# A router chain's scratch in PSUM, its gate folded away, and the norms' small steps on another engine

## The chip, the core and the metric

One core of a Trainium2 chip runs the whole program. TensorE (PE in the rows) multiplies matrices into PSUM, eight banks of 2 KB per partition; VectorE (DVE) and ScalarE (ACT) compute from SBUF or PSUM; GpSimd (POOL) computes from SBUF; SyncE (SP) issues transfers. The metric is device microseconds of one launch, lower is better.

## The reference

The input x is 8 batches of 512 channels by 2048 positions, in float32. Two layers, each added to x through a gate:

```python
x = x + tanh(g_xattn[0]) * xattn(layernorm(x), ctx, mask, ...)
x = x + tanh(g_ffn[0]) * ffn(layernorm(x), router_weight, router_bias, expert_bias)
```

xattn: windows of 128 positions; q and k from the normalised x (512 to 256 channels), v from ctx, 8 heads of 32, softmax, times v, exact gelu, back to 512 channels. ffn, for each of the 4096 rows of a length of 2048:

```python
logits = flat @ router_weight.T + router_bias          # 64 experts
scores = softmax(logits)
topk_w, topk_idx = top_k(scores, 8)
w_sum = topk_w.sum(-1, keepdims=True)
w_dense = zeros.at[rows, topk_idx].add(topk_w)
out = flat * w_sum + w_dense @ expert_bias
```

With flat = (x - m) * rstd, the second layer is x * (1 + t*w_sum*rstd) - t*w_sum*rstd*m + t*(w_dense @ expert_bias), with t = tanh(g_ffn). The factor, the shift and the mix are what the lines around the change compute.

## The kernel before

A unit is 256 positions of one batch: 8 units a batch, 64 in all. The order of all work is written as a table of lags, SLOTS: a unit starts every 16 slots, and each engine walks through the same ticks (8 to a slot) and emits what is due. A batch takes 128 slots. ENDS shifts the last units. Each engine has its own instruction stream in this order, and semaphores join them.

For a unit, GpSimd normalises x to z32 (z_full, L1051), ScalarE rounds it to z_hi, GpSimd takes the rest z_lo (z_low, L1058), and TensorE makes q and k from three products each (L310 to L312). ctx is split likewise (cx_hi L599, cx_lo L1064), and v_mm (L325 to L327) makes v, which ScalarE takes out of PSUM (v_full, L605). Scores (L341, L349), row maxima (top, L766), exponentials (L615, in four groups), transposes of P in 32x32 blocks on VectorE (turn_p, L773), the denominators (L778, L782), sixteen transfers that regroup the blocks to PT (move, L521; SyncE waits there for the division of the unit before), the product with v (L366), the division (divide, L788), gelu (L631), a split into ot_hi (L640) and ot_lo (L1075), the output projection (L385 to L387), its evacuation (L801) and GpSimd's add into x (L1070). Then the new x is transposed (L404), split (L647, L831) and multiplied by the router weights into the bank PR (L417, L418); bn_stats (L814) gathers mean and variance.

Once per batch, after its last unit, comes the router chain, amid the work of the next batch's first units. norm2 on VectorE: bn_aggr (L819), the negated mean (L823), variance plus eps (L824); on GpSimd the power -0.5 (L1079), which gives rstd in ln2[:, 2, :]. c_gate on VectorE: gate[0] = rstd * tanh(g_ffn) (L839) and gate[1] = gate[0] * -mean (L841). ScalarE copies PR to L (c_logits, L653), TensorE turns it into a bank called LT (c_turn, L428), of which the first 256 of 512 columns are used. c_top: logits times rstd plus bias (L847), the eight largest (L852), negation of the largest (L857), marking of the eight (match_replace L859, not_equal L862) in the SBUF tile lr. ScalarE takes the exponentials (c_exp, L658). c_weights: reciprocal of the sum (L866), masked weights (L868), normalised and doubled into w2 (L872). c_scale: sum of the weights (L877), times the two gates (L880, L881), plus one (L883), which signals ac. TensorE transposes w2 (w_turn, L439), ScalarE and VectorE split it (wt_hi L665, wt_lo L889), ScalarE scales x (L673), TensorE mixes the expert biases (L454, L455), VectorE adds (add_mix, L900), SyncE stores (L531) and later loads the batch after next (L526).

The statistics of the next batch's input go the same way: bn_aggr (L922), negated mean and variance plus eps on VectorE (L926, L927), the power on GpSimd (L1084).

Seven PSUM banks form a ring. take() gives each product the bank that is planned to be free first, by the table's due times, and notes the semaphore and count of that bank's last reader; TensorE waits for just this before it writes. So the planned end of a bank's use changes which bank the next products get and whom they wait for:

```python
at, i, last_reader, k = min(free)
...
free.append((t + round(8 * held), i, freed_by, n))
```

## Time and profile before

| | us |
|---|---|
| median of 3 runs | 1210.87 |
| lowest, highest | 1206.91, 1213.17 |
| profiled execution | 1210.61 |
| its span | 1208.5 |

| engine | busy us | share |
|---|---|---|
| TensorE, matmuls | 1126.1 | 93% |
| ScalarE | 1029.2 | 85% |
| VectorE | 975.5 | 81% |
| GpSimd | 707.7 | 59% |

The span's mean granted clock of TensorE was 0.985 of full speed. Matmuls are pipelined, so their busy time is not time at their peak; where TensorE stands still is read from its waits. A duration of an instruction includes the time that it stands after it has started. In a timeline a row can be several instructions of one line (x3), and the note in brackets is the engine's idle time before it and what ended it. SPq rows are SyncE's issuing of transfers.

### The profile page before, as it was taken

To read this page: it belongs to the slowest core of one execution; us is meant where nothing else is said; L and a number is where in the kernel's file an instruction comes from. 1 tells how busy PE (TensorE), PEld (TensorE's weight loads), DVE (VectorE), ACT (ScalarE), POOL (GpSimd) and SP (SyncE) were. 2 spreads that over 40 slices of the span, in tenths; PEclk is the share of its full clock that TensorE was granted. 3 is DMA by queue.
4 is the path that set the end of the run, shared out by engine and by line. 5 is a ranking of instruction groups with operands and counts; after the bars stand their busy time and mean duration, and the time that the engine had idled before them with its cause. 6 is when DMAs were issued, how large, how long until landed. Compare 5 with 4: busy or idle time off the path is not lost.

```text
span 1208.5 us, 33324 instructions
## 1 busy us (share of the span) xinstructions
PE 1126.1 (93%) x11661; PEld 1046.1 (87%) x11661; DVE 975.5 (81%) x1882; ACT 1029.2 (85%) x3200; POOL 707.7 (59%) x660
## 2 busy tenths in 40 slices
PE   2699999989999899999999999999999989999977
PEld 2699999889988899898998999988998889989965
DVE  6658878988789777998779887898779977797757
ACT  4688999888989799988998889898998879998954
POOL 2366677466655577466764666746764647746621
PEclk9899999999999999999999999999999989999989
DMA  9267554775548844487556965478554884456433
GB/s 287 74 175 199 143 130 116 237 201 155 132 112 252 218 124 123 117 270 209 131 129 187 235 169 131 119 233 217 141 131 121 253 215 124 125 137 203 110 92 139
DMA packets 169766, 199.82 MB, mean 165 GB/s; under 512 B 27776, under 2 KB 104704, under 8 KB 169472
## 3 DMA queue, kind: packets, MB, share of 16 engines
q1 hardware_dynamic: 168448, 197.20, 59.8%
q8 instruction: 93, 1.52, 0.6%
q10 hardware_dynamic: 1152, 0.50, 0.2%
q14 instruction: 73, 0.60, 0.2%
HBM read 80.06 MB, written 33.65 MB: 94 GB/s over the span
## 4 chain that ended last, share of the span: by engine, by line
PE 56%; SPq 21%; DVE 10%; issue 4%; ACT 4%; DMA 3%; POOL 1%; DVEq 0%; ACTq 0%; POOLq 0%
SPq L521 13%; PE ring L310 7%; PE ring L312 7%; PE ring L311 7%; DVE X L900 4%; PE ring L366 4%; SPq L526 4%; PE ring L325 3%; PE ring L327 3%; PE ring L326 3%; PE ring L349 3%; PE ring L385 3%; PE ring L387 3%; PE ring L386 3%; PE ring L404 3%
## 5 line engine op out<-in xcount | busy, mean ns | idle before, releaser
L615 ACT ACTIVATE P<-ring,nmx 128x128 f32<-128x128 f32 x1024 | 358.6, 402 | 30.9 <-DVE nmx L766 30.3
L310 PE MATMUL ring<-z_hi,wqk_hi 128*128 128x256 f32 x1024 | 299.8, 293 | 24.3 <-DVE z_lo L965 22.0
L311 PE MATMUL ring<-z_hi,wqk_lo 128*128 128x256 f32 x1024 | 292.4, 286 | 0.0
L312 PE MATMUL ring<-z_lo,wqk_hi 128*128 128x256 f32 x1024 | 292.3, 285 | 0.0
L615 ACT ACTIVATION_READ_ACCUMULATOR P<-ring,nmx 128x1 f32 x1024 | 248.5, 243 | 0.0
L1058 POOL TENSOR_TENSOR z_lo<-z,z_hi 128x1024 fp32r<-128x1024 f32 x62 | 147.6, 2381 | 167.5 <-ACT z_hi L583 167.5
L310 PEld LDWEIGHTS ring<-z_hi,wqk_hi 128*128 128x128 f32 x1024 | 198.5, 194 | 37.2 <-DVE wqk_lo L940 21.9
L1070 POOL TENSOR_TENSOR X<-X,xt 128x512 f32<-128x512 f32 x128 | 165.5, 1293 | 67.7 <-DVE xt L801 67.6
L773 DVE STREAM_TRANSPOSE T<-P 128x512 f32<-128x512 f32 x256 | 169.2, 690 | 44.2 <-ACT P L615 24.0
L311 PEld LDWEIGHTS ring<-z_hi,wqk_lo 128*128 128x128 f32 x1024 | 198.9, 194 | 0.0
L312 PEld LDWEIGHTS ring<-z_lo,wqk_hi 128*128 128x128 f32 x1024 | 198.9, 194 | 0.0
L1064 POOL TENSOR_TENSOR cx_lo<-cx,cx_hi 128x512 fp32r<-128x512 f32 x128 | 165.1, 1290 | 38.8 <-ACT cx_hi L599 38.7
L1075 POOL TENSOR_TENSOR ot_lo<-o,ot_hi 128x512 fp32r<-128x512 f32 x63 | 81.5, 1294 | 165.7 <-ACT ot_hi L640 165.7
L766 DVE TENSOR_REDUCE nmx<-ring 128x4 f32<-128x512 f32 x256 | 158.6, 682 | 16.7 <-PE ring L349 16.7
L325 PE MATMUL ring<-wv_hi,cx_hi 128*128 128x256 f32 x512 | 146.3, 286 | 8.1 <-POOL cx_lo L1064 8.1
L385 PE MATMUL ring<-ot_hi,wo_hi 128*128 128x256 f32 x504 | 143.1, 284 | 10.7 <-POOL ot_lo L1075 10.7
L801 DVE SCALAR_TENSOR_TENSOR xt<-ring,cst,mg 128x256 f32<-128x256 f32 x256 | 111.4, 477 | 45.0 <-PE ring L387 42.9
L326 PE MATMUL ring<-wv_lo,cx_hi 128*128 128x256 f32 x512 | 145.4, 284 | 0.0
L327 PE MATMUL ring<-wv_hi,cx_lo 128*128 128x256 f32 x512 | 145.4, 284 | 0.0
L387 PE MATMUL ring<-ot_lo,wo_hi 128*128 128x256 f32 x504 | 142.7, 283 | 0.0
L386 PE MATMUL ring<-ot_hi,wo_lo 128*128 128x256 f32 x504 | 142.2, 282 | 0.0
L1051 POOL TENSOR_SCALAR z<-X,ln 128x256 f32<-128x256 f32 x252 | 137.7, 562 | 0.7
(137 smaller groups left out, 2697.3 us busy)
## 6 DMA issues: line engine op xcount, KB each, us to landing
PT<-T SPq DMA_DIRECT2D x1018, 80.0 KB, 2.1
cx<-in_ctx SPq DMA_DIRECT2D x128, 256.0 KB, 3.9
out_y<-X SPq DMA_DIRECT2D x128, 256.0 KB, 3.1
X<-in_x SPq DMA_DIRECT2D x112, 256.0 KB, 4.6
mg<-in_mask SPq DMA_DIRECT2D x64, 128.0 KB, 3.2
X<-in_x SPq DMA_DIRECT2D x8, 512.0 KB, 8.5
sel<-rows_d SPq DMA_DIRECT2D x256, 3.0 KB
X<-in_eb SPq DMA_DIRECT2D x2, 512.0 KB, 7.7
```

The source lines that it names most:

```text
L310: e.matmul(o, wqk_hi[:, t, cols], z_hi[:, t, :], t == 0, False)
L311: e.matmul(o, wqk_lo[:, t, cols], z_hi[:, t, :], False, False)
L312: last = e.matmul(o, wqk_hi[:, t, cols], z_lo[:, t, :], False, t == DT - 1)
L325: e.matmul(o, cx_hi[:, k, :], wv_hi[:, k, :], k == 0, False)
L326: e.matmul(o, cx_hi[:, k, :], wv_lo[:, k, :], False, False)
L327: last = e.matmul(o, cx_lo[:, k, :], wv_hi[:, k, :], False, k == DT - 1)
L385: e.matmul(o, wo_hi[:, m, cols], o_hi[:, m, :], m == 0, False)
L386: e.matmul(o, wo_lo[:, m, cols], o_hi[:, m, :], False, False)
L387: last = e.matmul(o, wo_hi[:, m, cols], o_lo[:, m, :], False, m == 1)
L615: last = e.activation(P[:, n, :], bank("S", 4 * u + g)[:, k * W:(k + 1) * W], ACT.Exp, bias=nmx[u % 2][:, n:n + 1], accum_out=den[u % 2][: ...
L773: e.transpose(T[u % 2][:, :, 4 * g:4 * g + 4, :].rearrange("p b k i -> p k b i"), P[:, 4 * g:4 * g + 4, :].rearrange("p k (b j) -> p k b j ...
L1070: e.tensor_tensor(xs, xs, xt[j][:], ALU.add).then_inc(x1_g, 1)
```

## The change

The tile lr goes: the marks of the eight largest and the masked weights are written to the unused half of the logits' bank LT, low(b), and c_scale's two intermediate results to the bank's first columns. So LT is held until ac instead of lg: in the plan until c_sc (40.75) instead of c_top (38.75).

c_gate goes with its two instructions. c_scale forms the gain t * w_sum * rstd by one scalar_tensor_tensor from w_sum, tanh(g_ffn) and rstd, and the shift by another from the gain, -1 and the mean. It still has four instructions.

The negations of the mean and the additions of eps leave VectorE. In norm2 GpSimd adds eps before the power, and the negated mean is no longer formed. In input_norm GpSimd adds eps, negates the mean into nm1, and takes the power; z is still x plus the negated mean, times rstd. mv has two buffers now. Everything not shown below follows from this: names of semaphores, the place in the ticks where c_gate stood, and the operands of z (nm1 and rs1 for ln).

```diff
-    norm2=27.5, c_gate=33.5, L=36, LT=34, c_top=38.75, c_exp=37.75, c_w=40.75, c_sc=40.75, wT=43, wt_hi=43.25, wt_lo=42.25, mix=43.75, m_gap=0.25,
+    norm2=27.5, L=36, LT=34, c_top=38.75, c_exp=37.75, c_w=40.75, c_sc=40.75, wT=43, wt_hi=43.25, wt_lo=42.25, mix=43.75, m_gap=0.25,
...
-        mv = sb("mv", [128, DT, 2])
+        mv = [sb(f"mv{i}", [128, DT, 2]) for i in range(2)]
         bn2 = sb("bn2", [128, DT, 4, 6])
         mv2 = sb("mv2", [128, DT, 2])
-        ln1 = [sb(f"ln1_{i}", [128, 3, DT]) for i in range(2)]
-        ln2 = sb("ln2", [128, 3, DT])
+        rs1 = [sb(f"rs1_{i}", [128, DT]) for i in range(2)]
+        nm1 = [sb(f"nm1_{i}", [128, DT]) for i in range(2)]
+        rs2 = sb("rs2", [128, DT])
...
-        lr = sb("lr", [128, DT, NX])
...
-        gate = sb("gate", [128, 2, DT])
...
             for b in batch(t, C["LT"]):
-                take(("LT", b), t, C["c_top"] - C["LT"], lg_v, b + 1)
+                take(("LT", b), t, C["c_sc"] - C["LT"], ac_v, b + 1)
...
             def norm2(b):
                 e.wait_ge(bn2_v, 16 * (b + 1))
+                if b:
+                    e.wait_ge(ac_v, b)
                 for t in range(DT):
                     e.bn_aggr(mv2[:, t, :], bn2[:, t, :, :].rearrange("p a c -> p (a c)")).then_inc(agg2_v, 1)
-                if b:
-                    e.wait_ge(ac_v, b)
-                e.wait_ge(agg2_v, DT * (b + 1))
-                e.tensor_scalar(ln2[:, 0, :], mv2[:, :, 0], -1.0, None, ALU.mult).then_inc(neg2_v, 1)
-                e.tensor_scalar(ln2[:, 1, :], mv2[:, :, 1], EPS, None, ALU.add).then_inc(neg2_v, 1)
...
-            def c_gate(b):
+            def c_top(b):
                 if b == 0:
                     e.wait_ge(sm_rb, 16)
                     e.wait_ge(sm_small, 96)
-                e.wait_ge(neg2_v, 2 * b + 2)
-                e.wait_ge(rstd2_g, b + 1)
-                e.tensor_scalar(gate[:, 0, :], ln2[:, 2, :], cst[:, TF:TF + 1], None, ALU.mult).then_inc(dm_v, 1)
-                e.wait_ge(dm_v, b + 1)
-                e.tensor_tensor(gate[:, 1, :], gate[:, 0, :], ln2[:, 0, :], ALU.mult).then_inc(gate_v, 1)
-
-            def c_top(b):
                 e.wait_ge(rstd2_g, b + 1)
                 e.wait_ge(lt_pe, b + 1)
                 for t in range(DT):
                     last = e.scalar_tensor_tensor(out=lg[:, t, :], in0=bank("LT", b)[:, t * NX:(t + 1) * NX],
-                                                  scalar=ln2[:, 2, t:t + 1], in1=rbb[:], op0=ALU.mult, op1=ALU.add)
+                                                  scalar=rs2[:, t:t + 1], in1=rbb[:], op0=ALU.mult, op1=ALU.add)
                 last.then_inc(lg_v, 1)
                 e.wait_ge(lg_v, b + 1)
                 for t in range(DT):
...
                 e.wait_ge(t8_v, b + 1)
                 e.tensor_scalar(sc[:, :, 0:1], t8[:, :, 0:1], -1.0, None, ALU.mult).then_inc(neg_v, 1)
                 for t in range(DT):
-                    last = e.match_replace(lr[:, t, :], t8[:, t, :], lg[:, t, :], -3.0e38)
+                    last = e.match_replace(low(b)[:, t, :], t8[:, t, :], lg[:, t, :], -3.0e38)
                 last.then_inc(mr_v, 1)
                 e.wait_ge(mr_v, b + 1)
-                e.tensor_tensor(lr[:], lr[:], lg[:], ALU.not_equal).then_inc(sel_v, 1)
+                e.tensor_tensor(low(b), low(b), lg[:], ALU.not_equal).then_inc(sel_v, 1)
+
+            def low(b):
+                return bank("LT", b)[:, DT * NX:2 * DT * NX].rearrange("p (t x) -> p t x", t=DT)
 
             def c_weights(b):
                 e.wait_ge(ex_a, b + 1)
                 e.reciprocal(sc[:, :, 3:4], sc[:, :, 1:2]).then_inc(wm_v, 1)
                 e.wait_ge(sel_v, b + 1)
-                e.tensor_tensor(ex[:], ex[:], lr[:], ALU.mult).then_inc(wm_v, 1)
+                e.tensor_tensor(low(b), low(b), ex[:], ALU.mult).then_inc(wm_v, 1)
                 if b:
                     e.wait_ge(wT_pe, b)
                 e.wait_ge(wm_v, 4 * b + 2)
-                e.tensor_tensor(w2[:], ex[:].unsqueeze(2).to_broadcast([128, DT, 2, NX]),
+                e.tensor_tensor(w2[:], low(b).unsqueeze(2).to_broadcast([128, DT, 2, NX]),
                                 sc[:, :, 3:4].unsqueeze(3).to_broadcast([128, DT, 2, NX]), ALU.mult).then_inc(w2_v, 1)
 
             def c_scale(b):
                 e.wait_ge(w2_v, b + 1)
-                e.tensor_reduce(sc[:, :, 5:6], w2[:, :, 0, :], AX.X, ALU.add).then_inc(wm_v, 1)
-                e.wait_ge(gate_v, b + 1)
+                wsum, gain = bank("LT", b)[:, 0:DT], bank("LT", b)[:, DT:2 * DT]
+                e.tensor_reduce(wsum, w2[:, :, 0, :], AX.X, ALU.add).then_inc(wm_v, 1)
                 e.wait_ge(wm_v, 4 * b + 3)
-                e.tensor_tensor(sc[:, :, 4:5], sc[:, :, 5:6], gate[:, 0, :].unsqueeze(2), ALU.mult).then_inc(wm_v, 1)
-                e.tensor_tensor(sc[:, :, 7:8], sc[:, :, 5:6], gate[:, 1, :].unsqueeze(2), ALU.mult)
+                e.scalar_tensor_tensor(out=gain, in0=wsum, scalar=cst[:, TF:TF + 1], in1=rs2[:], op0=ALU.mult,
+                                       op1=ALU.mult).then_inc(wm_v, 1)
                 e.wait_ge(wm_v, 4 * b + 4)
-                e.tensor_scalar(sc[:, :, 6:7], sc[:, :, 4:5], 1.0, None, ALU.add).then_inc(ac_v, 1)
+                e.scalar_tensor_tensor(out=sc[:, :, 7], in0=gain, scalar=-1.0, in1=mv2[:, :, 0], op0=ALU.mult, op1=ALU.mult)
+                e.tensor_scalar(sc[:, :, 6], gain, 1.0, None, ALU.add).then_inc(ac_v, 1)
 
             def w_low(b):
...
             def input_norm(b):
-                ln = ln1[b % 2]
                 e.wait_ge(bn1_v, 16 * (b + 1) - 4)
-                if b:
-                    e.wait_ge(rstd1_g, b)
                 if b >= 2:
                     e.wait_ge(z32_g, NU * (b - 1) + 1)
                 for t in range(DT):
                     if b or t != TA:
-                        e.bn_aggr(mv[:, t, :], bnst[:, t, :, :].rearrange("p a c -> p (a c)")).then_inc(agg1_v, 1)
-                if b == 0:
-                    e.wait_ge(st_a, 6)
-                e.wait_ge(agg1_v, DT * (b + 1) - 1)
-                e.tensor_scalar(ln[:, 0, :], mv[:, :, 0], -1.0, None, ALU.mult).then_inc(neg1_v, 1)
-                e.tensor_scalar(ln[:, 1, :], mv[:, :, 1], EPS, None, ALU.add).then_inc(neg1_v, 1)
+                        e.bn_aggr(mv[b % 2][:, t, :], bnst[:, t, :, :].rearrange("p a c -> p (a c)")).then_inc(agg1_v, 1)
...
             def norm2(b):
-                e.wait_ge(neg2_v, 2 * (b + 1))
-                e.tensor_tensor(ln2[:, 2, :], ln2[:, 1, :], half[:], ALU.pow).then_inc(rstd2_g, 1)
+                e.wait_ge(agg2_v, DT * (b + 1))
+                e.tensor_scalar(rs2[:], mv2[:, :, 1], EPS, None, ALU.add).then_inc(eps2_g, 1)
+                e.wait_ge(eps2_g, b + 1)
+                e.tensor_tensor(rs2[:], rs2[:], half[:], ALU.pow).then_inc(rstd2_g, 1)
 
             def input_norm(b):
-                ln = ln1[b % 2]
-                e.wait_ge(neg1_v, 2 * (b + 1))
-                e.tensor_tensor(ln[:, 2, :], ln[:, 1, :], half[:], ALU.pow).then_inc(rstd1_g, 1)
+                if b == 0:
+                    e.wait_ge(st_a, 6)
+                e.wait_ge(agg1_v, DT * (b + 1) - 1)
+                e.tensor_scalar(rs1[b % 2][:], mv[b % 2][:, :, 1], EPS, None, ALU.add).then_inc(eps1_g, 1)
+                e.tensor_scalar(nm1[b % 2][:], mv[b % 2][:, :, 0], -1.0, None, ALU.mult).then_inc(eps1_g, 1)
+                e.wait_ge(eps1_g, 2 * b + 2)
+                e.tensor_tensor(rs1[b % 2][:], rs1[b % 2][:], half[:], ALU.pow).then_inc(rstd1_g, 1)
```

VectorE, around norm2 and c_gate of the second batch, with the semaphores that each row waits for. Before:

```order
338 L823 TENSOR_SCALAR ln<-mv 128x4 [waits s_agg2,s_ac]
339 L824 TENSOR_SCALAR ln<-mv 128x4
340 L801 SCALAR_TENSOR_TENSOR xt<-ring,cst,mg 128x256 [waits s_WO,s_mg0,s_x1]
341 L801 SCALAR_TENSOR_TENSOR xt<-ring,cst,mg 128x256
342 L766 TENSOR_REDUCE nmx<-ring 128x4 [waits s_S,s_exp]
343 L766 TENSOR_REDUCE nmx<-ring 128x4 x3
344 L839 TENSOR_SCALAR gate<-ln,cst 128x4 [waits s_rstd2,s_neg2]
345 L841 TENSOR_TENSOR gate<-gate,ln 128x4 [waits s_dm]
346 L801 SCALAR_TENSOR_TENSOR xt<-ring,cst,mg 128x256 [waits s_WO,s_x1]
347 L801 SCALAR_TENSOR_TENSOR xt<-ring,cst,mg 128x256
348 L773 STREAM_TRANSPOSE T<-P 128x4x4x32 [waits s_exp,s_pt] x3
349 L847 SCALAR_TENSOR_TENSOR lg<-ring,ln,rbb 128x64 [waits s_LT,s_rstd2]
```

The same stretch now:

```order
328 L800 SCALAR_TENSOR_TENSOR xt<-ring,cst,mg 128x256 [waits s_WO,s_mg0,s_x1]
329 L800 SCALAR_TENSOR_TENSOR xt<-ring,cst,mg 128x256
330 L765 TENSOR_REDUCE nmx<-ring 128x4 [waits s_S,s_exp]
331 L765 TENSOR_REDUCE nmx<-ring 128x4 x3
332 L800 SCALAR_TENSOR_TENSOR xt<-ring,cst,mg 128x256 [waits s_WO,s_x1]
333 L800 SCALAR_TENSOR_TENSOR xt<-ring,cst,mg 128x256
334 L772 STREAM_TRANSPOSE T<-P 128x4x4x32 [waits s_exp,s_pt] x3
335 L836 SCALAR_TENSOR_TENSOR lg<-ring,rs,rbb 128x64 [waits s_LT,s_rstd2]
```

Four small instructions are gone from between the others; the rest stands in the same order.

TensorE, in the first batch's router chain: the first matmul of a v projection, the transposes of w2, the first matmul of an output projection. Before:

```order
1223 L325 MATMUL ring<-wv_hi,cx_hi 128x256 [waits s_cxlo,s_cxhi,s_lg]
...
1235 L439 MATMUL ring<-ident,w 128x128 [waits s_w2,s_on]
1236 L439 MATMUL ring<-ident,w 128x128 x3
1237 L385 MATMUL ring<-ot_hi,wo_hi 128x256 [waits s_otlo,s_v]
```

The same rows now:

```order
1223 L324 MATMUL ring<-wv_hi,cx_hi 128x256 [waits s_cxlo,s_cxhi,s_on]
...
1235 L438 MATMUL ring<-ident,w 128x128 [waits s_w2,s_v]
1236 L438 MATMUL ring<-ident,w 128x128 x3
1237 L384 MATMUL ring<-ot_hi,wo_hi 128x256 [waits s_otlo,s_ac]
```

No matmul moved; the three have exchanged banks, and with them the readers for whom they wait: s_on is the division's, s_v the eviction of v, s_ac the end of c_scale.

GpSimd, at norm2. Before:

```order
91 L1075 TENSOR_TENSOR ot_lo<-o_0,ot_hi 128x512 [waits s_othi]
92 L1079 TENSOR_TENSOR ln<-ln,half 128x4 [waits s_neg2]
93 L1058 TENSOR_TENSOR z_lo<-z,z_hi 128x1024 [waits s_zhi,s_qk]
```

And now:

```order
95 L1056 TENSOR_TENSOR ot_lo<-o_0,ot_hi 128x512 [waits s_othi]
96 L1060 TENSOR_SCALAR rs<-mv 128x4 [waits s_agg2]
97 L1062 TENSOR_TENSOR rs<-rs,half 128x4 [waits s_eps2]
98 L1039 TENSOR_TENSOR z_lo<-z,z_hi 128x1024 [waits s_zhi,s_qk]
```

One instruction stands ahead of the power, and the power waits for it.

## Rows read from the trace of the kernel before

**Rows 1.** The page's first part: busy us, share of the span, instructions.
```profile
PE 1126.1 (93%) x11661; PEld 1046.1 (87%) x11661; DVE 975.5 (81%) x1882; ACT 1029.2 (85%) x3200; POOL 707.7 (59%) x660
```

**Rows 2.** Waits of TensorE, 60 to 1150: total us, times, longest.
```profile
PE ring L366 <- DMA PT<-T: 17.7, 12, 3.7
PE ring L385 <- POOL ot_lo L1075: 8.5, 8, 1.2
PE ring L454 <- DVE wt_lo L889: 5.9, 7, 1.0
```

**Rows 3.** The chain that ended last, 505 to 522: start, us, what.
```profile
516.75 1.93 DVE X L900 x3
518.68 0.48 SPq L531
```

**Rows 4.** Timeline of VectorE, 491 to 509: start, us, line, operation.
```profile
491.85 0.96 DVE L839 TENSOR_SCALAR gate<-ln,cst 128x4 f32<-128x4 f32 x1
492.84 1.21 DVE L841 TENSOR_TENSOR gate<-gate,ln 128x4 f32<-128x4 f32 x1
493.98 0.86 DVE L801 SCALAR_TENSOR_TENSOR xt<-ring,cst,mg 128x256 f32<-128x256 f32 x2
...
496.58 0.81 DVE L847 SCALAR_TENSOR_TENSOR lg<-ring,ln,rbb 128x64 f32<-128x64 f32 x4
...
501.31 0.65 DVE L788 TENSOR_TENSOR o<-ring,PT 128x512 f32<-128x512 f32 x1
...
503.79 1.24 DVE L881 TENSOR_TENSOR sc<-sc,gate 128x4 f32<-128x4 f32 x1
...
506.81 0.68 DVE L889 TENSOR_TENSOR wt_lo<-ring,wt_hi 128x512 fp32r<-128x512 f32 x1
508.44 0.69 DVE L900 TENSOR_TENSOR X<-X,ring 128x512 f32<-128x512 f32 x1 [0.96 <-PE ring L455]
```

**Rows 5.** Timeline of GpSimd, 489 to 509.
```profile
489.15 2.39 POOL L1058 TENSOR_TENSOR z_lo<-z,z_hi 128x1024 fp32r<-128x1024 f32 x1
...
492.74 1.30 POOL L1064 TENSOR_TENSOR cx_lo<-cx,cx_hi 128x512 fp32r<-128x512 f32 x1
...
503.71 1.30 POOL L1075 TENSOR_TENSOR ot_lo<-o,ot_hi 128x512 fp32r<-128x512 f32 x1 [4.11 <-ACT ot_hi L640]
```

**Rows 6.** Timeline of ScalarE, 491 to 509.
```profile
494.74 0.28 ACT L615 ACTIVATION_READ_ACCUMULATOR P<-ring,nmx 128x1 f32 x1
...
502.00 0.91 ACT L631 ACTIVATE o<-o,cst 128x256 f32<-128x256 f32 x2 [0.63 <-DVE o L788]
...
505.94 2.13 ACT L673 ACTIVATE X<-X,sc 128x2048 f32<-128x2048 f32 x1
```

**Rows 7.** Timeline of TensorE, 491 to 509.
```profile
491.70 0.35 PE L310 MATMUL ring<-z_hi,wqk_hi 128*128 128x256 f32 x1
...
494.63 1.00 PE L428 MATMUL ring<-id,L 128*128 128x64 f32 x8
...
505.15 0.36 PE L385 MATMUL ring<-ot_hi,wo_hi 128*128 128x256 f32 x1 [1.21 <-POOL ot_lo L1075]
...
507.64 0.47 PE L454 MATMUL ring<-eb,wt_hi 128*128 128x512 f32 x1 [0.81 <-DVE wt_lo L889]
```

**Rows 8.** Two lines by source: ns min/median/max, first and last start.
```profile
L841 DVE TENSOR_TENSOR gate<-gate,ln x8: 165/1211/1212, 203.2 to 1186.8; 128x4 f32<-128x4 f32 x8
...
L862 DVE TENSOR_TENSOR lr<-lr,lg x8: 426/706/711, 209.6 to 1189.8; 128x256 f32<-128x256 f32 x8
```

**Rows 9.** Groups of VectorE by line and shape: busy us, mean ns, idle before.
```profile
L900 DVE TENSOR_TENSOR X<-X,ring 128x512 f32<-128x512 f32 x128 | 79.4, 681 | 9.4 <-PE ring L455 9.3
...
L872 DVE TENSOR_TENSOR w<-ex,sc 128x512 f32<-128x512 f32 x8 | 5.5, 692 | 0.8
```

**Rows 10.** Groups of GpSimd by line and shape.
```profile
L1051 POOL TENSOR_SCALAR z<-X,ln 128x256 f32<-128x256 f32 x252 | 137.7, 562 | 0.7
...
L1097 POOL MEMSET half<- 128x4 f32 x1 | 0.1, 101 | 0.0
```

More of the change, by code:

```diff
@@ L196, in gated_block_kernel @@
         out_done = [[sem(f"out{t}{c}") for c in range(4)] for t in range(DT)]
-        bn1_v, agg1_v, neg1_v, rstd1_g = (sem(n) for n in ("bn1", "agg1", "neg1", "rstd1"))
+        bn1_v, agg1_v, eps1_g, rstd1_g = (sem(n) for n in ("bn1", "agg1", "eps1", "rstd1"))
         st_a = sem("st")
@@ L203, in gated_block_kernel @@
         gelu_a, othi_a, otlo_g, wo_pe, xt_v, x1_g = (sem(n) for n in ("gelu", "othi", "otlo", "WO", "xt", "x1"))
[L204 to L207 removed]
+        bn2_v, agg2_v, eps2_g, rstd2_g, ht_pe, hthi_a, htlo_v, r_pe = (sem(n) for n in (
+            "bn2", "agg2", "eps2", "rstd2", "hT", "hthi", "htlo", "R"))
+        l_a, lt_pe, lg_v, t8_v, neg_v, mr_v, sel_v, ex_a, w2_v, ac_v = (sem(n) for n in (
+            "L", "LT", "lg", "t8", "neg", "mr", "sel", "ex", "w2", "ac"))
         wm_v, wT_pe, wthi_a, wtlo_v, mix_pe, sx_a, x2_v = (sem(n) for n in (
@@ L957, in _ @@
                 for t in range(h.start, h.stop):
[L958 removed]
+                    last = e.tensor_scalar(z32[:, t, :], X[0][:, t, 0:U], nm1[0][:, t:t + 1], rs1[0][:, t:t + 1],
                                            ALU.add, ALU.mult)
@@ L1020, in _ @@
                         r_low(u, a)
-                for b in batch(t, C["c_gate"]):
-                    c_gate(b)
                 for b in batch(t, C["c_top"]):
@@ L1050, in z_full @@
                 for t in range(DT):
-                    last = e.tensor_scalar(z32[:, t, :], X[b % 2][:, t, c * U:(c + 1) * U], ln[:, 0, t:t + 1],
-                                           ln[:, 2, t:t + 1], ALU.add, ALU.mult)
+                    last = e.tensor_scalar(z32[:, t, :], X[b % 2][:, t, c * U:(c + 1) * U], nm1[b % 2][:, t:t + 1],
+                                           rs1[b % 2][:, t:t + 1], ALU.add, ALU.mult)
                 last.then_inc(z32_g, 1)
```

11 lines of the change are left out of this document (2 added, 9 removed).

## The prediction

> **What bounds the kernel now.** I read the page first: TensorE is busy for 93% of the span [rows 1], so time can only come out of places where it stands still or where its feeders set the pace. The waits of TensorE between 60 and 1150 us name three such places: 17.7 us behind the transfers of PT, 8.5 us where the output projection waits for ot_lo, 5.9 us where the mix waits for wt_lo [rows 2]. The last two happen once per batch, both in the some 17 us in which the router chain of the finished batch runs on VectorE. Then I read the chain that ended last around one such place: it leaves TensorE, passes VectorE's adds L900, and goes on in SyncE's queue [rows 3] until the wait for PT some 40 us later. So what the router chain delays on its way to L900 is paid by the whole kernel, also through the stretch where SyncE's issuing sets the pace: a store's issue there starts when L900 is done.
>
> Third, the timelines of the batch around 491 to 509 us. On VectorE [rows 4] nothing is idle from 491.85 to 507.5. Within that, L839 on 4 elements per partition takes 0.96 us and L841 1.21 us, and L881 takes 1.24 us. They are not slow by themselves: undisturbed, L841 takes 0.165 us and L862 0.43 us, against medians of 1.21 and 0.71 [rows 8]. GpSimd shows why [rows 5]: L841 ends as cx_lo ends (494.04), L881 as ot_lo ends (505.01); L839 stands in the same way before cx_lo begins. A VectorE instruction that needs what GpSimd is using stands until GpSimd's is over. Instructions with one operand in PSUM (L847, L788, L889, L900) never show this.
>
> The Trainium skill ("SBUF — State Buffer", Who interferes with whom) says the same: a VectorE instruction with two SBUF inputs contends with a GpSimd instruction that reads SBUF, one with at most one such input outside the two-port modes does not. The trace agrees (L841's 1.21 against 0.165 us, L900's even 0.68); by this rule the scratch in PSUM is out of the conflict's reach.
>
> **The change part by part, in that batch.**
>
> (a) Gate ops gone. VectorE goes straight on to L801: 493.98 becomes 491.85. The gain is not the whole 2.13 us, since others become late next. The third of the L773 transposes needs the third group of exponentials, whose last read ends at 495.02 [rows 6]; it would start at 495.1 and free VectorE at 495.7. L847 also needs L428, done at 495.63 [rows 7]. So L847 starts at 495.7 instead of 496.58: 0.88 us gained.
>
> (b) L862 gets an operand and its output in PSUM: 0.43 instead of 0.71 [rows 8], 0.27 gained with what rounding leaves. Together 1.15 us at L788 (501.31 to 500.16). ScalarE's gelu waits for that (0.63 us idle before 502.00 [rows 6]); its own table load before it moves with the exponentials, whose releaser L857 moves too. So gelu, ot_hi and ot_lo move by 1.15: ot_lo ends at 503.86 instead of 505.01. TensorE was free at 503.94 (505.15 less 1.21 idle [rows 7]), so L385 starts at 504.0: that wait goes.
>
> (c) After L788, L881's stall goes: 1.24 less some 0.17, 1.07 us. VectorE is then 2.2 us early, more than its suppliers. wt_hi on ScalarE moves by 1.15, wt_lo would end near 505.7 instead of 507.5, and L454 starts at about 505.8 instead of 507.64. The first L900 needs the scaled x as well: L673, 505.94 to 508.07 [rows 6], ends at 506.92 when it is 1.15 early. So L900 starts at 507.0 instead of 508.44 [rows 4]: **1.4 us gained** per batch at the point from which the chain runs on. SyncE's moves of PT wait for L788 too and start 1.15 early, and its stores waited for L900, so the queue follows.
>
> (d) This holds for seven of the eight batches. The last runs with GpSimd idle, without stalls, and its L847 waits for L428, not for the gate. Seven times 1.4 is 9.8. They are not quite alike (L841's median of 1.21 holds for nearly all, the exponentials end the same in each, but L847's start is not), so I take 9.4.
>
> (e) Negation and eps of norm2 leave VectorE, 0.33 us. VectorE then waits for L387 anyway: nothing. On GpSimd the eps comes between bn_aggr and the power: it costs one more small instruction, and saves the two on VectorE. The trace has no such GpSimd instruction; bounds are 0.10 us (memset of the same 128x4) and 0.56 (L1051, 256 elements) [rows 10]. With 0.1 for its semaphore, the power starts between 0.13 earlier and 0.33 later. Behind it is z_lo, 489.15 to 491.54 [rows 5], which TensorE needs at 491.70 [rows 7]: there is some 0.1 us of cover. Nearest is the memset, of the same size: I take 0.2, so 0 us; worst 0.2 times seven, 1.6 us.
>
> (f) input_norm: two small ops leave VectorE (one of them exposed to the same stall), and three small ones stand on GpSimd instead of one. It lies in the middle of a batch; no wait of TensorE for z is among those of rows 2, and the next batch's first z is used by TensorE only a unit later. Nothing, but for the start of the kernel, where x must be normalised before the first matmul: 0.1 lost (0 to 0.6, the same bounds).
>
> (g) Scratch in PSUM. Reading: L900 with an operand in PSUM takes 681 ns for 512 elements, L872 from SBUF alone 692 ns [rows 9], so about 0. Writing to PSUM by VectorE isn't in the trace; I bound it at -0.05 to 0.15 us an instruction (a whole small instruction, L841 at its least, takes 0.165, so more than that would double it). L859 and L862 lie before L788 in that way, with one exposed end each. I take 0.07 each, 0.15 per batch, 1.0 us in seven; bounds -0.7 to 2.1. Those after L788 have cover: ac would be ready near 502.9, the scaling needs it at 504.8. In the last batch they stand on the path: 0.2 (0 to 0.6).
>
> The Trainium skill ("VectorE: DVE Perf Modes", The TRN2 errata) speaks against this part: it gives a fixed 120 cycles from PSUM and 58 from SBUF, 65 ns at 0.96 GHz for each instruction that now reads PSUM, and advises to copy to SBUF where many operations follow. Rows 9 don't show that difference. By the page the sum would be about 0.3 us worse, since only L862 lies before L788.
>
> (h) The logits' bank is held longer, so three matmul groups take other banks. The v projection before w's transpose waits for L788 (on) instead of lg, the transpose L439 for v's eviction instead of on, and L385 for ac instead of v. TensorE's turns follow from its free moment, 503.94: between L385 and L454 twelve matmuls take 1.68 us [rows 7], 0.14 each, so the four transposes begin near 503.4 and the twelve of the projection near 501.7. In the new times L788 is done at 500.8, 0.9 before its turn. v's eviction follows ot_hi on ScalarE, now near 503.6; it moves to 502.5 and is done by 502.9, 0.5 before. ac comes at 502.9 (L881's end 505.03 less 2.15), 1.1 before 504.0. Nothing, then. Had L788 stayed (done at 501.96), the projection would wait 0.3 and the transposes 0.6, so this cover is lent by (a) and (b).
>
> **Sum.** 9.4 - 1.0 - 0.1 - 0.2 = 8.1 us from the profiled execution's 1210.6 (span 1208.5): **1202.5 us**. The median of the runs is 1210.87, 0.3 above that execution; the runs lie 6.3 apart, so 0.5% (6 us) is about what one can tell.
>
> **Rivals.**
>
> *The gain is taken back in the DMA stage.* TensorE waits up to 3.7 us for PT [rows 2] some 50 us after each router chain. If that wait depends on transfers whose times don't move, everything gained before is waited for there, and only what the adds push remains. For it: SyncE's queue sets the pace there. Against it: that stretch of the chain begins with a store released by L900 [rows 3], so it moves with it. Half kept: 1206.5. It counts as no change. Chance 0.22.
>
> *VectorE is freed, but ScalarE or the exponentials hold more than I think,* so that each batch gains only the ot_lo wait less a rest, 0.7 us: 4.9 - 1.3 = 3.6, 1207. Chance 0.10.
>
> *Slower: the PSUM chain holds L385.* L385 now waits for ac, the end of a dozen instructions of which each touches PSUM. At 504.0 it would have its turn; ac is expected at 502.9. If each of some 12 instructions costs 0.1 us more, the cover is gone; from 0.2 us each, ac comes at 505.3, after today's 505.15, and the mix is late with it. At 0.27 each: 7 x 1 = 7 us lost, 1217.5. Against it: reading PSUM is free in rows 9, and a write would have to double the time of a small instruction. Chance 0.06.
>
> *The change doesn't do what it says:* stalls persist because L857, with both operands in SBUF, falls on GpSimd's L1051 after the shift. At most 0.54 us there and none elsewhere: 7 x 0.5, 1206. Chance 0.07, no change.
>
> **Chances and range.** Forecast 0.55. Faster by over 0.5% (under 1204.8): 0.59, with a part of the last rival's and the DMA rival's spread. Within 0.5%: 0.33. Slower: 0.08. Range: the upper end takes in the partial gains and the bounds of (e) and (g), 1209; the lower end is the full 10 us with PSUM writes that cost nothing, and the runs' own spread, 1198.5.
>
> **What would show it.** In the profile after: no small VectorE instruction of the router chain over 0.5 us but perhaps L857's successor; TensorE's wait for ot_lo in seven batches near 0; L788's successor about 1.1 us earlier against the exponentials of its unit; the first mix add 1.4 us earlier. The waits for PT should stay near 18 us; if they rise to 25, the first rival holds. If TensorE waits for ac at L385's successor, the slower one holds. The prediction falls if the new small ops on GpSimd take more than 0.4 us each, for then TensorE's q projection waits for z_lo.

## The result and the profile after the change

The changed kernel takes 1200.51 us, the median of seven runs (1198.41 to 1203.66); the kernel before takes 1208.5 us on the same chip (median of seven, 1206.91 to 1213.17). The ratio is 0.9936 with a 95% interval of 0.9916 to 0.9956, so between 5.3 and 10.2 us are gained. The profiled execution took 1201.23 us, its span 1199.4 us.

The page's busy line of the changed kernel answers [rows 1]. VectorE has 48 instructions fewer and is busy 27.7 us less; GpSimd has 24 more and is busy 6.6 us more; TensorE is what it was.

```profile
PE 1127.4 (94%) x11661; PEld 1046.8 (87%) x11661; DVE 947.8 (79%) x1834; ACT 1029.4 (86%) x3200; POOL 714.3 (60%) x684
```

The waits of TensorE between 60 and 1150 us (total us, times, longest) answer [rows 2]:

```profile
PE ring L365 <- DMA PT<-T: 18.2, 13, 2.5
...
PE ring L453 <- DVE wt_lo L882: 1.5, 7, 0.2
PE ring L384 <- POOL ot_lo L1056: 0.4, 1, 0.4
```

The wait for ot_lo falls from 8.5 to 0.4 us, that for wt_lo from 5.9 to 1.5, and that for PT stays.

Absolute times differ between two profiles, so the router chain is read from a common mark: ScalarE's copy of the logits (L653, now L652), which begins the chain. In the batch of [rows 3 to 7] it starts at 491.62 before and at 487.74 after:

```profile
491.62 0.61 ACT L653 ACTIVATE L<-PR 128x512 f32<-128x512 f32 x1
```

```profile
487.74 0.61 ACT L652 ACTIVATE L<-PR 128x512 f32<-128x512 f32 x1
```

The timeline of VectorE after that mark in the changed kernel (start, us, line, operation), against [rows 4]:

```profile
491.88 0.84 DVE L836 SCALAR_TENSOR_TENSOR lg<-ring,rs,rbb 128x64 f32<-128x64 f32 x4
...
494.46 0.43 DVE L851 TENSOR_TENSOR ring<-ring,lg 128x256 f32<-128x256 f32 x1
...
496.30 0.65 DVE L787 TENSOR_TENSOR o<-ring,PT 128x512 f32<-128x512 f32 x1
...
498.66 0.23 DVE L872 SCALAR_TENSOR_TENSOR ring<-ring,cst,rs 128x4 f32<-128x4 f32 x1
498.92 0.17 DVE L875 SCALAR_TENSOR_TENSOR sc<-ring,mv 128x4 f32<-128x4 f32 x1
...
501.19 0.69 DVE L882 TENSOR_TENSOR wt_lo<-ring,wt_hi 128x512 fp32r<-128x512 f32 x1 [0.24 <-ACT wt_hi L664]
503.10 1.28 DVE L893 TENSOR_TENSOR X<-X,ring 128x512 f32<-128x512 f32 x2 [1.22 <-ACT X L672]
```

The logits' scaling (L836) starts 4.14 us after the mark instead of 4.96, the division (L787) 8.56 instead of 9.69, the first mix add (L893) 15.36 instead of 16.82. Between the first and the last of these rows no small instruction stands over 0.5 us. Before the first add VectorE now waits 1.22 us for the scaled x (L672), where it waited 0.96 us for TensorE [rows 4].

The timeline of GpSimd in the same stretch, against [rows 5]:

```profile
483.94 0.23 POOL L1060 TENSOR_SCALAR rs<-mv 128x4 f32<-128x4 f32 x1 [1.81 <-DVE mv L820]
484.26 1.04 POOL L1062 TENSOR_TENSOR rs<-rs,half 128x4 f32<-128x4 f32 x1
485.27 2.39 POOL L1039 TENSOR_TENSOR z_lo<-z,z_hi 128x1024 fp32r<-128x1024 f32 x1
...
494.06 1.28 POOL L1045 TENSOR_TENSOR cx_lo<-cx,cx_hi 128x512 fp32r<-128x512 f32 x1 [0.49 <-ACT cx_hi L598]
498.70 1.29 POOL L1056 TENSOR_TENSOR ot_lo<-o,ot_hi 128x512 fp32r<-128x512 f32 x1 [3.36 <-ACT ot_hi L639]
```

The comparison L851 runs from 494.46 and L875 from 498.92, both inside a GpSimd instruction (494.06 to 495.34, 498.70 to 499.99), and neither stands. z_lo is where it was in this batch, 2.47 us before the mark in both kernels (489.15 against 491.62, 485.27 against 487.74); only in the first and the second batch it comes later, by 0.08 and 0.35 us. ot_lo starts 1.13 us earlier against the mark.

Over the batches the gain at the first add is 1.37, 1.06, 1.46, 1.47, 1.56, 1.47 and 1.56 us, and nothing in the last. At the end of the sixteenth add it sums to 10.0 us. The spans differ by 9.1 us (1208.5 to 1199.4). What lies between 10.0 and the medians' 8.0 us is the question of the last experiments.

### The profile page after: what moved, and what is told of

It reads as the page before. It is cut to its first block, busy times and chain, and to the rows that moved or that the text cites. A ratio compares the mean times of both kernels' runs of the same rounds, so it can differ in the third digit from the quotient of the medians.

```text
span 1199.4 us, 33283 instructions
## 1 busy us (share of the span) xinstructions
PE 1127.4 (94%) x11661; PEld 1046.8 (87%) x11661; DVE 947.8 (79%) x1834; ACT 1029.4 (86%) x3200; POOL 714.3 (60%) x684
## 4 chain that ended last, share of the span: by engine, by line
PE 49%; SPq 24%; DVE 10%; ACT 7%; issue 5%; DMA 3%; POOL 2%; ACTq 0%; DVEq 0%; POOLq 0%
SPq L520 15%; PE ring L309 6%; PE ring L311 5%; PE ring L310 5%; SPq L525 4%; PE ring L365 3%; ACT P L614 3%; PE ring L348 3%; DVE X L893 3%; PE ring L384 3%; PE ring L385 3%; PE ring L386 3%; PE ring L324 3%; PE ring L325 3%; PE ring L326 3%
## 5 line engine op out<-in xcount | busy, mean ns | idle before, releaser
L614 ACT ACTIVATION_READ_ACCUMULATOR P<-ring,nmx 128x1 f32 x1024 | 251.3, 245 | 0.0
L772 DVE STREAM_TRANSPOSE T<-P 128x512 f32<-128x512 f32 x256 | 171.9, 694 | 59.8 <-ACT P L614 37.4
L1032 POOL TENSOR_SCALAR z<-X,nm,rs 128x256 f32<-128x256 f32 x252 | 138.2, 564 | 0.8
```

The source lines that it names most:

```text
L614: last = e.activation(P[:, n, :], bank("S", 4 * u + g)[:, k * W:(k + 1) * W], ACT.Exp, bias=nmx[u % 2][:, n:n + 1], accum_out=den[u % 2][: ...
L772: e.transpose(T[u % 2][:, :, 4 * g:4 * g + 4, :].rearrange("p b k i -> p k b i"), P[:, 4 * g:4 * g + 4, :].rearrange("p k (b j) -> p k b j ...
```

## The experiments

**The theory.** The gain is the stalls: VectorE instructions that need what GpSimd is using stand until GpSimd's is over. Taking the gate out removes two, and a PSUM operand removes those of L862 and L881. (The stall in c_scale is there in all of the first seven batches, but on L881 in four only: on L880 in two and on L883 in one.) **The rival** says that fewer instructions or less work do it, or that the PSUM part is worth nothing. The first four kernels do one part each.

**Only the gate gone.** c_scale keeps its SBUF operands and forms the gain and shift from w_sum, as the changed kernel does.

```diff
-                e.tensor_tensor(sc[:, :, 4:5], sc[:, :, 5:6], gate[:, 0, :].unsqueeze(2), ALU.mult).then_inc(wm_v, 1)
-                e.tensor_tensor(sc[:, :, 7:8], sc[:, :, 5:6], gate[:, 1, :].unsqueeze(2), ALU.mult)
+                e.scalar_tensor_tensor(out=sc[:, :, 4], in0=sc[:, :, 5], scalar=cst[:, TF:TF + 1], in1=ln2[:, 2, :], op0=ALU.mult,
+                                       op1=ALU.mult).then_inc(wm_v, 1)
...
+                e.tensor_tensor(sc[:, :, 7], sc[:, :, 4], ln2[:, 0, :], ALU.mult)
```

> Before, with the gate folded into c_scale alone; scratch stays in SBUF, the norms' small steps stay on VectorE. My theory (the first add of the mix is what the kernel's time follows): L847 and L788 come 0.8 us earlier per batch, the c_scale stall of some 1.1 us behind ot_lo stays, so wt_lo and the first add gain 0.8 us; seven batches give 5.6 us, so about 5 us off the kernel before. Rival 'only instructions count, stalls are hidden': two instructions of 0.17 us less in eight batches, 2.6 us at most. Rival 'all of it must be undone together' (nothing by itself): 0.

Measured: ratio 0.9961 (0.9933 to 0.9989). The gains at the first add are 0.35, 0.04, 0.39, 0.40, 0.49, 0.42 and 0.29 us, 2.4 in sum (and the last batch's add comes 0.46 us later in this profile). That is less than half of the 5.6 us that the theory had put down, and by its size it would fit the rival of at most 2.6 us. The rows speak against that rival: the scaling of the logits starts 0.8 us earlier, as the theory expected, and the two instructions undisturbed would make 0.34 of it. Three rows of VectorE and three of GpSimd, in the batch whose mark is at 488.22, show where the other half went:

```profile
494.91 1.17 DVE L854 TENSOR_TENSOR lr<-lr,lg 128x256 f32<-128x256 f32 x1
...
497.51 0.65 DVE L787 TENSOR_TENSOR o<-ring,PT 128x512 f32<-128x512 f32 x1
...
500.11 1.12 DVE L874 TENSOR_TENSOR sc<-sc,ln 128x4 f32<-128x4 f32 x1
```

```profile
490.59 1.29 POOL L1060 TENSOR_TENSOR X<-X,xt 128x512 f32<-128x512 f32 x1
...
494.53 1.27 POOL L1054 TENSOR_TENSOR cx_lo<-cx,cx_hi 128x512 fp32r<-128x512 f32 x1 [0.51 <-ACT cx_hi L598]
499.91 1.30 POOL L1065 TENSOR_TENSOR ot_lo<-o,ot_hi 128x512 fp32r<-128x512 f32 x1 [4.11 <-ACT ot_hi L639]
```

And the comparison and the same GpSimd rows in the kernel before:

```profile
499.18 0.70 DVE L862 TENSOR_TENSOR lr<-lr,lg 128x256 f32<-128x256 f32 x1
```

```profile
494.92 1.29 POOL L1070 TENSOR_TENSOR X<-X,xt 128x512 f32<-128x512 f32 x1 [0.89 <-DVE xt L801]
...
498.32 1.28 POOL L1064 TENSOR_TENSOR cx_lo<-cx,cx_hi 128x512 fp32r<-128x512 f32 x1
```

In both kernels the comparison ends 0.28 us after cx_lo (499.88 and 499.60; 496.08 and 495.80). But cx_lo moves less than VectorE does. In the kernel before it ended a run of GpSimd work that began with the add into x, and this add waited for VectorE's L801. Without the gate instructions the add comes 0.93 us earlier against the mark (2.37 instead of 3.30), but cx_lo only 0.39 (6.31 instead of 6.70), as it then waits for ScalarE's cx_hi. The comparison starts 0.87 us earlier against the mark and ends 0.40 earlier: it stands 1.17 instead of 0.70 us. Of the 0.8 us that the gate's removal won ahead of it, 0.4 are lost at once. L874 stands 1.12 us in the way that L881 did [rows 4].

**Only the scratch in PSUM.** The gate and the norms as before, lr in the bank.

```diff
-                    last = e.match_replace(lr[:, t, :], t8[:, t, :], lg[:, t, :], -3.0e38)
+                    last = e.match_replace(low(b)[:, t, :], t8[:, t, :], lg[:, t, :], -3.0e38)
...
-                e.tensor_tensor(sc[:, :, 4:5], sc[:, :, 5:6], gate[:, 0, :].unsqueeze(2), ALU.mult).then_inc(wm_v, 1)
+                e.tensor_tensor(gain, wsum, gate[:, 0, :], ALU.mult).then_inc(wm_v, 1)
```

> Before, with the scratch and c_scale's intermediate results in the logits' bank and nothing else; the two gate instructions stay, with their stalls. My theory: not_equal loses its 0.27 us stall before L788, c_scale its 1.1 us behind it. ScalarE and ot_lo gain only 0.27, the first add is then held by the scaling of x, which gains as much: 16.26 instead of 16.82 us after the copy of the logits, 0.5 to 0.6 us per batch, 3.5 to 4 us in all. TensorE's wait for ot_lo shrinks from 1.2 to 0.9 us. Rival 'PSUM writes are slow': no gain or a loss of up to 2 us, and rows of these instructions above 0.25 us for 4 elements.

Measured: ratio 0.9972 (0.995 to 0.9995). The division gains 0.27 us in a batch and the first add 0.55 to 0.71, 4.5 in sum at the last add, somewhat more than the expected 3.5 to 4. TensorE's wait for ot_lo shrinks further than expected, to 0.5 us at most instead of 0.9. The waits of TensorE in this kernel:

```profile
PE ring L384 <- POOL ot_lo L1078: 3.6, 7, 0.5
PE ring L340 <- DVE X L903: 3.0, 14, 0.2
PE ring L453 <- DVE wt_lo L892: 1.6, 7, 0.2
PE ring L438 <- ACT v L604: 1.2, 7, 0.2
```

The last row is the exchange of banks: the transposes of w wait 0.2 us for v's eviction, in seven batches. In the changed kernel this row is absent, so the cover that the prediction's (h) spoke of is indeed lent by the gate's removal. It had 0.6 us for a division that stays where it was; here the division is 0.27 us early, which leaves some 0.3, and 0.2 is measured.

**Only the norms' steps moved.**

```diff
-                e.tensor_scalar(ln2[:, 0, :], mv2[:, :, 0], -1.0, None, ALU.mult).then_inc(neg2_v, 1)
-                e.tensor_scalar(ln2[:, 1, :], mv2[:, :, 1], EPS, None, ALU.add).then_inc(neg2_v, 1)
...
+                e.tensor_scalar(rs2[:], mv2[:, :, 1], EPS, None, ALU.add).then_inc(eps2_g, 1)
+                e.wait_ge(eps2_g, b + 1)
+                e.tensor_tensor(rs2[:], rs2[:], half[:], ALU.pow).then_inc(rstd2_g, 1)
```

> Before, with negation and eps moved to GpSimd in both norms; gates (formed from the mean itself, by a multiplication with -1) and scratch as before. My theory: 0, within 1 us either way; z_lo may end 0.1 us later. Rival 'the stall of input_norm's first small instruction, 0.83 us in the middle of each batch, was paid': 4 to 6 us faster. Rival 'GpSimd's longer sequence delays z_lo': up to 2 us slower.

Measured: ratio 1.0 (0.998 to 1.0019). In its one profile the seven chains take 0.8 us more, nearly all of it in the second and third batch; the times show neither a gain nor a loss of more than 2.4 us. So this part is worth nothing that can be told.

**All but the scratch in PSUM.** The changed kernel with lr and c_scale's two results back in SBUF.

```diff
-                e.tensor_tensor(low(b), low(b), lg[:], ALU.not_equal).then_inc(sel_v, 1)
+                e.tensor_tensor(lr[:], lr[:], lg[:], ALU.not_equal).then_inc(sel_v, 1)
...
-                wsum, gain = bank("LT", b)[:, 0:DT], bank("LT", b)[:, DT:2 * DT]
+                wsum, gain = sc[:, :, 5], sc[:, :, 4]
```

> The changed kernel with the scratch and c_scale's results back in SBUF and the bank released as before; gate folded, norms on GpSimd. My theory: as the gate alone, 5 to 6 us off the kernel before, so 3 to 4 us slower than the changed kernel. In its trace c_scale stands for some 1.1 us behind ot_lo and not_equal 0.2 to 0.3 us. Rival 'PSUM brings nothing, the gate all': the time of the changed kernel, 8 us off.

Measured: ratio 0.9991 (0.9966 to 1.0017), and in the trace the local gains of the gate-only kernel again: 0.31, 0.04, 0.40, 0.41, 0.50, 0.41 and 0.51 us, 2.6 in sum, where the theory had 5 to 6. So the two parts don't add. Alone they gain 2.4 and 4.5 us, together 10.0. The missing 3.1 us are about seven times the 0.43 us that the comparison in SBUF takes from the gate's gain (0.83 us at the logits' scaling, 0.40 at the division). With an operand in PSUM the comparison takes 0.43 us wherever it falls, and only then is the gate's gain kept.

**Does the operand's place decide, by itself?** The next kernels were timed on another occasion, with the changed kernel beside them. This is the changed kernel once more:

> The changed kernel once more, beside the three that follow: 6 to 10 us faster than the kernel before.

Measured: ratio 0.9944 (0.9922 to 0.9965); first adds earlier by 1.37, 1.05, 1.45, 1.46, 1.55, 1.47 and 1.55 us, as in its first profile.

Two probes add one useless instruction of 4 elements per partition behind the comparison. It is the same operation in both; the first has both operands in SBUF:

```diff
+                e.tensor_tensor(spare[:], half[:], rbb[:, 0:DT], ALU.mult)
```

> The changed kernel with one useless VectorE instruction per batch added behind not_equal: a product of two SBUF tiles of 4 elements per partition, read by nobody. GpSimd's cx_lo runs there (494.06 to 495.34 us in the third batch). Theory 'two SBUF inputs stand behind GpSimd': its row reads 0.6 to 0.7 us, the fourth transpose and the division come 0.55 us later, the first add 0.55 later, seven batches 3.8 us slower than the changed kernel. Rival 'small instructions are slow only behind their own semaphore waits': 0.16 us, at most 0.7 us in all.

and the second has one in PSUM:

```diff
+                e.tensor_tensor(spare[:], bank("LT", b)[:, 0:DT], rbb[:, 0:DT], ALU.mult)
```

> The same useless instruction at the same place with one operand in PSUM (four columns of the logits' bank) and the other in SBUF. Theory 'two SBUF inputs stand behind GpSimd': 0.16 to 0.2 us, some 0.1 us later per batch, 0.7 us in all, so 3 us faster than the probe with two SBUF operands. Rival 'any instruction at that place stands': the same as that probe.

The groups of VectorE by line and shape (busy us, mean ns, idle before), the SBUF probe and then the PSUM probe:

```profile
L853 DVE TENSOR_TENSOR spare<-half,rbb 128x4 f32<-128x4 f32 x8 | 3.9, 488 | 0.0
```

```profile
L853 DVE TENSOR_TENSOR spare<-ring,rbb 128x4 f32<-128x4 f32 x8 | 1.2, 152 | 0.0
```

And the instruction itself in the third batch, beside GpSimd's, in the first probe:

```profile
494.21 0.56 DVE L853 TENSOR_TENSOR spare<-half,rbb 128x4 f32<-128x4 f32 x1
```

```profile
493.47 1.27 POOL L1047 TENSOR_TENSOR cx_lo<-cx,cx_hi 128x512 fp32r<-128x512 f32 x1 [0.49 <-ACT cx_hi L599]
```

In the second it runs from 493.39 for 0.15 us in the midst of cx_lo (492.65 to 493.93). The first ends at 494.77, as cx_lo ends (494.74). The division comes 0.49 us later than in the changed kernel with the first, 0.07 with the second; the seven chains together lose 3.3 and 0.7 us. The ratios to before are 0.9963 (0.9944 to 0.9982) and 0.9949 (0.9923 to 0.9974). Their intervals overlap, so here the trace tells and the times only agree. In the last batch, where GpSimd is idle, the SBUF form takes 153 ns too: it is not slow by itself. The Trainium skill ("SBUF — State Buffer", Who interferes with whom) has this as its rule: a VectorE instruction with two SBUF inputs contends with a GpSimd instruction that reads SBUF, and its second input comes through the shared read interface. The trace agrees, with 0.56 against 0.15 us for one instruction.

**The bound that is next.** In the changed kernel the first add waits for the scaled x. This kernel scales the first 512 positions by themselves in every batch, not only in the last:

```diff
-                pieces = (slice(0, 512), slice(512, S)) if b == NB - 1 and t == 0 else (slice(0, S),)
+                pieces = (slice(0, 512), slice(512, S)) if t == 0 else (slice(0, S),)
```

> The changed kernel with ScalarE's first scaling of x per batch cut into 512 and 1536 elements, as the last batch already has it. Theory 'the first add is held by the scaling of x, no longer by TensorE': the first add comes 0.25 us earlier and is released by TensorE; 1 to 2 us faster than the changed kernel. Rival 'the adds follow something else, or ScalarE's extra instruction takes it back': no change or up to 1 us slower.

Measured: ratio 0.9925 (0.9898 to 0.9952), median 1200.47 us against the changed kernel's 1202.63 on this occasion. The two intervals overlap; it is the fastest of all kernels here, but not by a margin that the times can tell. The first add no longer waits for ScalarE but for TensorE's mix, and comes 1.7 us earlier than before instead of 1.46:

```profile
502.98 1.29 DVE L893 TENSOR_TENSOR X<-X,ring 128x512 f32<-128x512 f32 x2 [0.96 <-PE ring L454]
```

The chains gain 11.6 us in sum, 1.6 more than in the changed kernel, as the theory expected. But its span, 1200.4, is no shorter, and the wait for PT is the longest of all kernels:

```profile
PE ring L365 <- DMA PT<-T: 22.7, 16, 2.5
```

**Is part of the gain given back between the chains?** That was the prediction's first rival, and one profile of each kernel can't tell it. Two more profiles of each of the two kernels were taken, without any edit:

> The kernel before once more, for a second profile of it. In each profile the time between two router chains (from the last add of one to ScalarE's copy of the logits of the next) and the start vary; against the first profile of before, those of eight other kernels so far sum to between 2.9 us worse and 2.6 us better over the seven stretches. Theory A (the stretches between chains keep what a chain gains, the scatter is a profile's own): before differs from its own first profile by as much, within some 3 us in sum, of either sign, and by nothing within the seven chains (first add within 0.1 us in each). Theory B (part of a gain is given back in the waits for PT): nothing different for this kernel.

> The changed kernel's third profile. Local gain of the first adds against before 9.9 to 10.0 us in sum, as in its two others. Theory A: the stretches between the chains sum, over this kernel's profiles, to the same as over those of before, within 1.5 us. Theory B: they are together 2 to 5 us longer than before's.

> The kernel before, third profile: as for its second. With three profiles of before and four of the changed kernel the mean of the stretches between the chains can be compared: Theory A equal within 1.5 us, Theory B 2 to 5 us longer with the change.

> The changed kernel, fourth profile: as for its third. Theory A: span 1199 to 1202; Theory B the same span, but with before's spans in the same call near 1206 rather than near 1209.

Each profile is cut at fixed marks: the seven chains, from ScalarE's copy of the logits to the end of the sixteenth add, and the seven stretches from there to the next copy.

| profile | span | first mark | seven chains | seven stretches | TensorE idle in them |
|---|---|---|---|---|---|
| before | 1208.5 | 202.1 | 210.0 | 773.3 | 23.6 |
| before, 2nd | 1205.2 | 202.4 | 210.0 | 769.7 | 22.8 |
| before, 3rd | 1207.7 | 203.2 | 210.0 | 771.4 | 24.1 |
| changed | 1199.4 | 203.0 | 200.0 | 773.3 | 25.5 |
| changed, 2nd | 1200.8 | 201.5 | 200.1 | 776.1 | 26.8 |
| changed, 3rd | 1199.7 | 201.5 | 200.0 | 775.1 | 25.6 |
| changed, 4th | 1200.8 | 202.1 | 200.0 | 775.6 | 26.0 |

The last two columns come from the busy times of the seven stretches; the idle is the sum less PE. The three profiles of before, in the table's order:

```profile
sum 773.27, PE 749.70 PEld 706.31 DVE 613.06 ACT 676.82 POOL 500.60; mean PE 107.10 PEld 100.90 DVE 87.58 ACT 96.69 POOL 71.51
sum 769.72, PE 746.92 PEld 704.09 DVE 612.09 ACT 677.75 POOL 501.37; mean PE 106.70 PEld 100.58 DVE 87.44 ACT 96.82 POOL 71.62
sum 771.35, PE 747.23 PEld 704.21 DVE 612.72 ACT 677.26 POOL 500.71; mean PE 106.75 PEld 100.60 DVE 87.53 ACT 96.75 POOL 71.53
```

The four of the changed kernel:

```profile
sum 773.31, PE 747.83 PEld 704.98 DVE 606.86 ACT 677.64 POOL 505.41; mean PE 106.83 PEld 100.71 DVE 86.69 ACT 96.81 POOL 72.20
sum 776.13, PE 749.36 PEld 706.11 DVE 606.63 ACT 678.14 POOL 505.68; mean PE 107.05 PEld 100.87 DVE 86.66 ACT 96.88 POOL 72.24
sum 775.09, PE 749.46 PEld 706.53 DVE 606.74 ACT 677.67 POOL 505.50; mean PE 107.07 PEld 100.93 DVE 86.68 ACT 96.81 POOL 72.21
sum 775.59, PE 749.62 PEld 706.48 DVE 606.03 ACT 677.91 POOL 505.45; mean PE 107.09 PEld 100.93 DVE 86.58 ACT 96.84 POOL 72.21
```

The chains repeat to 0.1 us: the change takes 10.0 us out of them, every time. The stretches between are 3.6 us longer in the mean (775.0 against 771.4), with single profiles of one kernel up to 3.6 us apart. Of these 3.6 us TensorE stands idle 2.5, and there no profile of the changed kernel comes down to one of before.

The remaining 1.1 us are in its busy time, and they go with the granted clock, not with the kernel. The profiles with a mean clock of 0.985 or 0.986 over the span, one of before and three of the changed kernel, have 749.4 to 749.7 us busy in the stretches; the changed kernel's first, at 0.987, has 747.8; the other two of before, at 0.988 and 0.989, have 746.9 and 747.2, and the PSUM probe's, at 0.988, has 747.0.

By the waits of these stretches, 1.7 of the 2.5 us are for PT (15.3 against 17.0). So 10.0 - 3.6 + 0.5 (the first mark, within its scatter) = 6.9 us, the difference of the mean spans (1207.1 and 1200.2). It lies near the two differences of timed medians, 8.0 and 7.1 us. Theory B had 2 to 5 us, and the idle time speaks for it. Its sign on the spans can't be used: those of before on that occasion were 1205.2, 1207.7 and, of an execution without a profile here, 1211.4 us. Nor is theory A's 3 us for a profile's own scatter enough, as two profiles of before differ by 3.6. The kernel with the split scaling fits too: its stretches have 28.4 us idle, 2.4 more than the changed kernel's mean. They are only 0.7 us longer than that mean, though (775.7), and the rest of what its chains gain went with a first mark that came 1.1 us later. The other kernels' single profiles have 23.4 us idle (norms only), 23.9 (gate only), 25.0 (SBUF probe), 25.6 (scratch only) and 26.1 (all but the scratch). One profile stands against it: that of the PSUM probe, whose chains are nearly as short (200.7), has stretches of 770.7 us with 23.7 idle, like the kernel before. Counted with the four of the changed kernel it brings the difference in the stretches down to 2.7 us, 2.0 of them idle.

The timed executions give a second estimate, once the clock is taken into account. Beside the changed kernel's second profile 71 executions of five kernels were timed. The 29 of before have a mean clock of 0.9875, the twelve of the changed kernel one of 0.9858. A straight line through all 71, with one slope and an offset for each kernel, has a slope of 1.1 us for 0.001 of clock. At equal clock it puts the changed kernel 8.5 us ahead of before, the PSUM probe 8.2, the SBUF probe 5.6 (each with a standard error of 0.7) and the split scaling 9.1 (0.9). So the two probes differ by 2.6 us (0.8), which is what their chains differ by. The same fit on the first occasion has the gate alone 2.6 us ahead, the scratch alone 2.7, all but the scratch 0.9, and the norms alone 0.8 behind (0.7 each): by the times too the parts make clearly less than the whole. The 8.5 us stand against 10.0 in the chains and some 0.4 outside the span (an execution is 2.2 us longer than its span with the kernel before and 1.8 with the changed one), so about 1.9 us are missing.

So that something is given back is likely, and its size, some 2 to 2.5 us of 10.0, is open by about 1 us. What exactly holds the transfers in SyncE's queue there was not tried; that it is this queue is argued from the chain of before, not shown.

## Why the prediction was right, point by point

The forecast was a gain of 8.1 us and 1202.5 us; measured are 8.0 us between the medians (5.3 to 10.2 by the ratio) and 1200.51 us. The kernel before was itself at 1208.5 in these runs instead of 1210.87, and that is the 2 us between forecast and time. The total is right, but partly by luck, because two errors are of opposite sign.

- **What bounds the kernel** was read right: the last two rows of [rows 2] shrink by 12.5 us in sum, that for PT stays, and what the first add gains goes on to the end.
- **(a)** 0.88 us ahead of the logits' scaling: 0.82. The gate-only kernel shows the same 0.8. What the prediction didn't see is that without (b) half of it would be lost again behind cx_lo, which follows VectorE by only 0.39 us. As both parts are in the change, no term suffered.
- **(b)** 1.15 at the division: 1.13; the comparison takes 432 ns in all eight batches, against 706 in the median of [rows 8]. The wait for ot_lo went.
- **(c)** The stall of c_scale went (L875 takes 166 ns in the mean). The prediction read it as L881's; in three of the seven batches it was on L880 or L883, with 1.19 to 1.28 us, which makes no difference to the sum. The first add is held by the scaled x, as foreseen: 1.46 us for 1.4.
- **(d)** Seven batches and nothing in the last (0.02 us later): 10.0 at the last adds for 9.4. The allowance for unlike batches was needed mainly for the second, whose chain gains 1.06: there L839 had stood only 0.61 us instead of 0.96, so there was less to gain.
- **(e)** The new GpSimd instruction takes 234 ns for a guess of 200, and z_lo does not move in five of the seven batches (0.08 and 0.35 us in the other two); the kernel with the norms alone shows no loss that its times can tell. Nothing, then, as forecast, within some 1 us.
- **(f)** The start: the first mark comes at 202.1 to 203.2 before and 201.5 to 203.0 after. 0.1 us can't be told.
- **(g)** The write to PSUM is the term that was mis-sized. It was put at 0.07 us an instruction, 1.2 us in all, for want of a row. The rows after, by line and shape, are these:

```profile
L848 DVE MATCH_REPLACE8 ring<-t,lg 128x64 f32<-128x64 f32 x32 | 6.4, 217 | 0.0
...
L860 DVE TENSOR_TENSOR ring<-ring,ex 128x256 f32<-128x256 f32 x8 | 3.3, 406 | 0.0
...
L864 DVE TENSOR_TENSOR w<-ring,sc 128x512 f32<-128x512 f32 x8 | 5.5, 692 | 0.8
```

  The first two took 204 and 394 ns with their output in SBUF, so writing costs 0.01 us. The third reads PSUM and takes the 692 ns that it took from SBUF [rows 9]. The Trainium skill ("VectorE: DVE Perf Modes", The TRN2 errata) would put 65 ns on an instruction that reads PSUM; the trace does not show it. The prediction's 0.3 us for this is also mis-summed: seven times 65 ns is 0.45 us, without the last batch.
- **(h)** Nothing, and the second experiment shows that the cover is real: without it the wait appears, at 0.2 us.

**The rivals.** The one that took half the gain back in the DMA stage was right in kind and too large. The sum charged nothing there, and likely some 2 to 2.5 us of 10.0 are given back. The step that then failed is the argument that the stretch "begins with a store released by L900, so it moves with it". The total came out all the same because the sum was 1.8 us too low in the chains and the tail, (d) and (g) together (8.2 without the start, against 10.0), which covers most of it. The expected sign in the profile was blunt: PT's wait was to stay near 18 or rise to 25, and one profile gave 18.2. Over all profiles in that window it is 17.7, 17.0 and 20.4 before, 18.2, 19.1, 19.5 and 19.4 after, and no single one could have told. The partial gain of 0.7 us a batch is refuted by the timeline. The slower case, TensorE waiting for ac, has no row in any profile. Against what the last rival had, L857's successor L846 doesn't stand: it starts at 493.47, only 0.1 us before GpSimd's z ends (493.57), and takes 172 ns in the mean, where L857 took 240 in that batch.
